# A two-layer gated cross-attention block: the first expert layer computed for every expert, and for the routed expert only

## The chip, the cores and the metric

One NeuronCore of one Trainium2 chip. The metric is the device time of one launch in microseconds. The kernel is written engine by engine: TensorE (PE), VectorE (DVE), ScalarE (ACT), GpSimd (POOL) and SyncE (SP), each with its own instruction order, and semaphores between them.

## The reference, cut to what matters

Eight batches of 256 rows of 256 numbers pass through two layers, each a gated cross-attention and a gated expert layer (`D` = 256, eight experts). Layer 0's expert layer takes one expert per row:

```python
x = x + tanh(g_xattn[0]) * L0_xattn(layernorm(x), ctx)      # bidirectional attention, one head, gated mix
x = x + tanh(g_ffn[0])   * L0_ffn(layernorm(x))
x = x + tanh(g_xattn[1]) * L1_xattn(layernorm(x), ctx, ctx) # 16 heads of 16, rotary embedding
x = x + tanh(g_ffn[1])   * L1_ffn(layernorm(x))             # 8 experts of 128, the best 2 per row

def L0_ffn(x):
    logits = x @ router_w.T + router_b
    probs = softmax(logits)
    top1 = argmax(probs)
    y_all = einsum('bsd,eod->bseo', x, expert_w) + expert_b
    return y_all[top1] * max(probs)
```

## The kernel before, in words

All of `x` stays on the chip in `xall` [128, 8, 2, 256]: batch, two row tiles of 128, 256 columns. Most products are made as three fp32r matmuls of a high and a low part (`mm3`, lines 298 to 301: hi*hi, hi*lo, lo*hi); so every operand is split, high part by ACT (`*_hi`), low part by DVE or POOL (`*_lo`). Weights are loaded by SP into one of four `stage` buffers, and split into `wA` (attention) or `wB` (the eight layer-0 experts, later layer 1's f and p).

The order of work is written out by hand, once per engine, as a list of calls under conditions on `k`. There are two loops. The first (`k` from -1 to 9) is a software pipeline of layer 0: iteration `k` makes the projections, scores and softmax of batch `k`, PV, gate, mix and the second layer norm ("B") with the routing of batch `k`-1, and the experts of batch `k`-2. `k` = 8 and 9 only drain it, and start layer 1's attention for batch 0 (`c_qk(0)` in `k` = 9). The second loop (`k` from 1 to 11) is layer 1: `c_qk`/`c_v` of batch `k`, `c_max` (scores once, for the row maxima) of batch `k`-1, `c_exp`/`c_PV` (scores again, transposed, with the maxima as three more rows of the contraction) of batch `k`-2, output projection and layer norm "D" of `k`-3, and the expert layer `d_up`/`d_down` of `k`-4. The last batch's experts 1 to 7 stand in its first iteration.

Layer 0's experts: `expert(x, b)` takes a pair of experts (`p = x // 2`) and one row tile (`t = x % 2`) and writes 128 rows by two experts' 256 columns, six matmuls of 512 columns. All eight experts are computed for all rows: eight calls per batch. `add_expert` on DVE (line 1221) then adds each expert's 256 columns to `xall`, scaled by `gat`, which is the softmax's maximum where the expert is the chosen one and zero elsewhere. The bias goes in as a product of the transposed gates with the eight bias rows (`gT`, `bias`, `add_bias`). `b_top` (DVE) picks the best expert.

Names for the steps below: `ln_apply` (line 1093) writes the normalized rows; `out_f`, `out_hi`, `out_lo` take PV from PSUM on ACT, DVE and POOL before `gate`; `sum_diff` (POOL) and `gated` (DVE) prepare `mix`; `mixed` adds it to `xall`. In layer 1 `swap_halves` (SP, line 1757) exchanges halves of q and k by DMA for the rotation, `turned` (DVE and POOL) rotates, `part0` to `part2` split into three bf16 parts, `stack` (SP, line 1770) copies them to `st_` with twelve DMAs, `max_parts` and `max_rows` (line 1777) bring the row maxima there with three. PSUM's eight banks are handed out in rings (`take`); a bank is waited for by its next taker.

## Time and profile before

| | us |
|---|---|
| median of 3 runs | 680.89 (680.26 to 686.58) |
| the profiled execution | 681.88 |
| its span, first to last instruction | 679.9 |
| busy in the span: PE / weight loads / DVE / ACT / POOL | 561.5 / 476.3 / 525.0 / 301.1 / 220.6 |
| instructions | 11549 |
| moved by DMA | 34.31 MB |

Busy times are unions of intervals. A matmul's listed duration is longer than its step to the next one, because matmuls are pipelined; the start of the next instruction tells what one costs. "[0.24 <-POOL rstd L1595]" behind an instruction is the idle time of its engine before it and the releaser. SPq is SP's DMA-issuing queue.

### The profile page before, as it was taken

The numbers are of one execution on the slowest core, as the hardware profiler recorded it, in microseconds if no ns is written. First come the engines' busy times: TensorE is split into PE (matmuls) and PEld (weight loads), VectorE is DVE, ScalarE is ACT, GpSimd is POOL, SyncE is SP. The second block draws the span as 40 slices with busy tenths as digits, with TensorE's granted clock in tenths as the row PEclk, the third lists the DMA queues.
The fourth block names the chain that finished last, engine by engine and source line by source line (L and its number), as shares of the span: only waits on it lengthen the run. The fifth ranks groups of instructions, "written<-read, shape, count | busy, mean of one in ns | idle before, by whom it ended". The sixth has DMA issues, their size and how long they took to land.

```text
span 679.9 us, 11549 instructions
## 1 busy us (share of the span) xinstructions
PE 561.5 (83%) x4240; PEld 476.3 (70%) x4240; DVE 525.0 (77%) x1279; ACT 301.1 (44%) x629; POOL 220.6 (32%) x225
## 2 busy tenths in 40 slices
PE   3778999999999999464646758889897988797977
PEld 3677899898999997353433545768685776676777
DVE  3688988888888779774746748797988969687576
ACT  2536343433343443121114637565655655455622
POOL 2340413222231303311605434452726344212123
PEclk9998999999999999797886879999999989899989
DMA  5233010101000100018184643508081451700000
GB/s 190 78 94 93 1 32 1 32 2 63 1 1 1 63 1 1 15 31 116 24 118 116 113 60 57 87 24 135 0 101 43 57 85 24 88 2 18 16 1 31
DMA packets 25720, 34.31 MB, mean 50 GB/s; under 512 B 3648, under 2 KB 16704, under 8 KB 25664
## 3 DMA queue, kind: packets, MB, share of 16 engines
q1 hardware_dynamic: 25664, 33.58, 25.8%
q8 instruction: 33, 0.54, 0.4%
q14 instruction: 23, 0.19, 0.1%
HBM read 14.50 MB, written 2.10 MB: 24 GB/s over the span
## 4 chain that ended last, share of the span: by engine, by line
PE 44%; DVE 21%; SPq 10%; DMA 8%; issue 8%; ACT 5%; POOL 4%; DVEq 0%; POOLq 0%; ACTq 0%
PE psum L299 12%; PE psum L301 12%; PE psum L300 12%; SPq L1770 8%; DMA st<-mpt 6%; DVE mpad L1246 4%; DVE xn L1093 4%; PE psum L306 2%; PE psum L462 2%; DVE xall L1334 2%; PE psum L447 2%; PE psum L473 1%; DVE qr L1231 1%; SPq L1777 1%; DVE wB L1069 1%
## 5 line engine op out<-in xcount | busy, mean ns | idle before, releaser
L1246 DVE TENSOR_REDUCE mpad<-psum 128x2 f32<-128x512 f32 x128 | 84.0, 682 | 43.7 <-PE psum L447 43.6
L852 ACT ACTIVATE PT<-psum 128x512 f32<-128x512 f32 x128 | 72.3, 595 | 33.9 <-PE psum L462 32.0
L462 PE MATMUL psum<-st 99*128 99x256 bf16 x256 | 47.5, 286 | 30.3 <-DMA st<-mpt 23.6
L447 PE MATMUL psum<-st 96*128 96x256 bf16 x256 | 50.7, 293 | 23.4 <-DVE mpad L1246 14.3
L1221 DVE SCALAR_TENSOR_TENSOR xall<-psum,gat,xall 128x256 f32<-128x256 f32 x128 | 61.3, 479 | 6.2 <-PE psum L301 3.3
L1642 POOL TENSOR_TENSOR wA<-stage,wA 128x512 fp32r<-128x512 f32 x24 | 30.8, 1283 | 88.9 <-ACT wA L890 64.2
L299 PE MATMUL psum<-wB,x2h 128*128 128x512 f32 x128 | 53.5, 418 | 1.0 <-DVE xall L1221 1.0
L447 PEld LDWEIGHTS psum<-st 96*128 96x128 bf16 x256 | 19.8, 104 | 45.4 <-DVE mpad L1246 29.4
L462 PEld LDWEIGHTS psum<-st 99*128 99x128 bf16 x256 | 19.7, 101 | 45.5 <-DMA st<-mpt 25.0
L1334 DVE SCALAR_TENSOR_TENSOR xall<-psum,gat,xall 128x256 f32<-128x256 f32 x112 | 47.9, 474 | 4.5 <-PE psum L301 3.3
L1093 DVE TENSOR_SCALAR xn<-xall,mv,rstd 128x256 f32<-128x256 f32 x64 | 46.3, 764 | 6.5 <-POOL rstd L1595 6.5
L301 PE MATMUL psum<-wB,x2l 128*128 128x512 f32 x128 | 51.1, 399 | 0.0
L300 PE MATMUL psum<-wB,x2h 128*128 128x512 f32 x128 | 51.1, 399 | 0.0
L1600 POOL TENSOR_TENSOR cl<-cx,ch 128x512 fp32r<-128x512 f32 x14 | 17.9, 1278 | 86.3 <-ACT ch L742 86.2
L1588 POOL TENSOR_SCALAR ve<-mv 128x2 f32<-128x2 f32 x32 | 6.9, 217 | 114.7 <-DVE mv L1077 114.7
L299 PE MATMUL psum<-wB,wA 128*128 128x256 f32 x128 | 41.8, 327 | 2.6 <-DVE xall L1334 2.3
L306 PE MATMUL psum<-ident,xn 128*128 128x128 f32 x128 | 21.0, 290 | 24.4 <-DVE xn L1093 24.4
L881 ACT ACTIVATE stage<-psum 128x512 f32<-128x512 f32 x32 | 19.1, 598 | 44.7 <-PE psum L301 44.5
L299 PE MATMUL psum<-x4h,wB 128*128 128x256 f32 x128 | 37.8, 295 | 0.1
L300 PE MATMUL psum<-wB,wA 128*128 128x256 f32 x128 | 36.7, 287 | 0.0
L473 PE MATMUL psum<-PT,vv 128*32 128x256 f32 x512 | 35.1, 393 | 1.6 <-ACT PT L852 1.5
L301 PE MATMUL psum<-wB,wA 128*128 128x256 f32 x128 | 36.5, 285 | 0.0
(237 smaller groups left out, 1938.6 us busy)
## 6 DMA issues: line engine op xcount, KB each, us to landing
st<-parts SPq DMA_DIRECT2D x96, 128.0 KB, 5.6
stage<-mats_d SPq DMA_DIRECT2D x29, 256.0 KB, 4.1
cx<-ctx_d SPq DMA_DIRECT2D x16, 256.0 KB, 2.8
qr<-qp SPq DMA_DIRECT2D x16, 256.0 KB, 5.1
xall<-x_d SPq DMA_DIRECT2D x8, 256.0 KB, 3.0
out_d<-xall SPq DMA_DIRECT2D x8, 256.0 KB, 4.4
st<-mpt SPq DMA_DIRECT2D x24, 8.0 KB, 5.7
rope<-rope_d SPq DMA_DIRECT2D x1, 256.0 KB, 3.0
```

Of the source, the lines that this page charges most:

```text
L299: e.matmul(out, lhs[0], rhs[0], start=start, stop=False)
L300: e.matmul(out, lhs[0], rhs[1], start=False, stop=False)
L301: return e.matmul(out, lhs[1], rhs[0], start=False, stop=stop)
L447: last = e.matmul(o[:, t * 256:(t + 1) * 256], s[0:96, 0, h, t * 128:(t + 1) * 128], s[0:96, 1, h, :], start=True, stop=True)
L462: last = e.matmul(o[:, k * 256:(k + 1) * 256], s[0:99, 1, h, k * 128:(k + 1) * 128], s[0:99, 0, h, :], start=True, stop=True)
L473: last = e.matmul(o[32 * j:32 * j + 32, c:c + 256], vv[b % 3][:, k, h, :], PT[:, (H * b + h) % 6, k, :], start=(k == 0), stop=(k == 1))
L852: e.activation(flat(PT[:, n % 6, :, :]), ps("ST", b, h), ACT.Exp, scale=0.25).then_inc(a_ST, 1)
L1093: last = e.tensor_scalar(xn[:, i, t, :], xall[:, b, t, :], mv[:, i, t, 0:1], rstd[:, i, t:t + 1], ALU.subtract, ALU.mult)
L1221: e.scalar_tensor_tensor(out=xall[:, b, t, :], in0=ps("ffn", b, x)[:, i * 256:(i + 1) * 256], scalar=gat[:, b % 2, t, 2 * p + i:2 * p + i ...
L1246: e.tensor_reduce(mpad[:, :, h:h + 1], ps("max", b, h).rearrange("p (a n) -> p a n", a=2), AX, ALU.max, negate=True).then_inc(v_max, 1)
L1334: e.scalar_tensor_tensor(out=xall[:, b, t, :], in0=ps("dn", b, x)[:, t * 256:(t + 1) * 256], scalar=gat[:, b % 2, t, x:x + 1], in1=xall[:, ...
L1770: e.dma_start(st_[b % 2][16 * c:16 * c + 16, i, :, :], parts[:, i, p, :, :].rearrange("p o n -> p (o n)")).then_inc(d_stack, 16)
```

## The change

Layer 0's rows are sorted by expert on the chip, in three groups of 2, 3 and 3 batches (`GROUPS`). `b_top` writes the one-hot choice to `oh`. `rank(g)` counts, by products with a triangular matrix and a matrix of ones, how many earlier rows chose the same expert; `alloc(g)` gives every expert as many tiles of 128 slots as it needs and every row its slot, and every tile its expert. POOL's `scatter(g)` writes the normalized rows to a DRAM buffer `slots_d` by indirect DMA (128 rows of 1 KB each). Then each of the group's `2n+7` tiles (11, 13 and 13, enough for any routing) is loaded (`xs`), with its expert's weights and bias (`wt`, 768 columns, picked by a register read from `tile_e`), transposed, multiplied in plain fp32 (`moe_T`, `xs_T`, `moe_w`), the bias added (`y_out`), and stored to `y_d`; `gather(b)` brings the rows back and `add_moe(b)` adds them to `xall`, scaled. Three buffers of each go round. Slots that no row fills are zero at the start (`zero_slots`). Routing of layer 0 is now a plain fp32 product (`route_B`) straight to rows by experts. The experts' split copies, `gpad`, `gT`, `bias` and `x_lo` of B are gone; the new tiles share SBUF with `wB`, which layer 1 fills later.

Both loops become one, `k` from -1 to 20, with a new order on every engine. PV and `out` of batch `k` now stand in iteration `k`, `proj("qc")` an iteration earlier; `c_qk(0)` stands in `k` = 8, `c_max` of batch `k`-9, `c_exp` of `k`-10, `c_out` of `k`-11, `d_up` of `k`-12. `rank`/`scatter`: `k` = 2/3, 6/6, 8/9. Tiles 0 to 10 are multiplied in `k` = 4 to 6, 11 to 23 in `k` = 6 to 8, 24 to 36 in `k` = 10 and 11. `gather`: 0 and 1 in `k` = 6, 2 and 3 in 8, 4 in 9, 5 to 7 in 11.

```diff
-            def expert(x, b, ring="all"):
-                o = take(ring, "ffn", b, x)
-                p, t = x // 2, x % 2
...
-                for k in range(2):
-                    last = mm3(o.rearrange("p (a n) -> p a n", a=2), hl(x2[b % 2], lambda a: a[:, k, t * 128:(t + 1) * 128]),
-                               hl(wB, lambda a: a[:, 2 * p:2 * p + 2, k * 256:(k + 1) * 256]), k == 0, k == 1)
...
+GROUPS = [2, 3, 3]
+ROWT = [2 * n for n in GROUPS]
+TILES = [n + E - 1 for n in ROWT]
...
+            def rank(g, ring="all"):
+                o = take(ring, "rank", g)
+                w.wait_ge(v_oh, FIRST[g + 1])
...
+                e.matmul(o[:, 0:n * E], tri[:, :], oh[:, g, 0:n, :].rearrange("p a e -> p (a e)"), start=True, stop=False)
+                for i in range(ROWT[g]):
+                    last = e.matmul(o[:, (i + 1) * E:n * E].rearrange("p (a e) -> p a e", e=E), ones[:, :],
+                                    oh[:, g, i:i + 1, :].broadcast_to([128, n - 1 - i, E]), start=False, stop=(i == n - 2))
+            def moe_T(n, ring="all"):
+                o = take(ring, "moe", n)
+                w.wait_ge(d_xs[n % 3], 16 * (n // 3 + 1))
+                for k in range(2):
+                    last = e.transpose(o[:, k * 128:(k + 1) * 128], xs[:, n % 3, k * 128:(k + 1) * 128], ident[:, :])
+            def moe_w(n):
+                o = ps("moe", n)
+                w.wait_ge(a_xs, n + 1)
+                w.wait_ge(d_wt[n % 3], 16 * (n // 3 + 1))
+                for k in range(2):
+                    last = e.matmul(o[:, 256:512], xsT[:, n % 2, k, :], wt[:, n % 3, k * 256:(k + 1) * 256], start=(k == 0), stop=(k == 1))
+            def y_out(n):
+                w.wait_ge(t_moe, n + 1)
+                w.wait_ge(d_ys[n % 3], 16 * (n // 3))
...
+                e.tensor_tensor(ys[:, n % 3, :], ps("moe", n)[:, 256:512], wt[:, n % 3, 512:768], ALU.add).then_inc(v_ys, 1)
+            def add_moe(b):
+                w.wait_ge(d_yg[b % 2], 32 * (b // 2 + 1))
+                w.wait_ge(p_gat, 2 * b + 2)
+                for t in range(2):
+                    e.scalar_tensor_tensor(out=xall[:, b, t, :], in0=yg[:, b % 2, t, :], scalar=gatB[:, b, t:t + 1], in1=xall[:, b, t, :],
+                                           op0=ALU.mult, op1=ALU.add).then_inc(v_acc, 1)
+            def scatter(g):
+                w.wait_ge(v_slot, g + 1)
+                w.wait_ge(d_zero, 32)
+                w.wait_ge(t_xs, TILE0[max(g - 1, 0)])
+                for i in range(ROWT[g]):
+                    e.indirect_dma_start(slots_d[g % 2][0:128 * TILES[g], :], bass.IndirectOffsetOnAxis(ap=slot[:, g, i:i + 1], axis=0),
+                                         xB[:, (FIRST[g] + i // 2) % 5, i % 2, :], None).then_inc(d_slots, 16)
+            def gather(b):
+                g = GROUP[b]
+                for i in range(3):
+                    w.wait_ge(d_ys[i], 16 * ((TILE0[g + 1] + 2 - i) // 3))
+                w.wait_ge(v_acc, 2 * (b - 1))
+                for t in range(2):
+                    i = 2 * (b - FIRST[g]) + t
+                    e.indirect_dma_start(yg[:, b % 2, t, :], None, y_d[g % 2][0:128 * TILES[g], :],
+                                         bass.IndirectOffsetOnAxis(ap=slot[:, g, i:i + 1], axis=0)).then_inc(d_yg[b % 2], 16)
+            def load_tile(n):
+                g, j = tile_at(n)
+                w.wait_ge(v_tile, 2 * g + 2)
+                w.wait_ge(v_ys, n - 2)
+                at = e.value_load(tile_e[0:1, g, j:j + 1], min_val=0, max_val=E - 1)
+                e.dma_start(wt[:, n % 3, :], exp_d[bass.ds(at, 1), :, :].rearrange("a p n -> p (a n)")).then_inc(d_wt[n % 3], 16)
+                w.wait_ge(d_slots, 32 * FIRST[g + 1])
+                w.wait_ge(t_xs, n - 2)
+                e.dma_start(xs[:, n % 3, :], slots_d[g % 2][128 * j:128 * (j + 1), :]).then_inc(d_xs[n % 3], 16)
+            def store_tile(n):
+                g, j = tile_at(n)
+                w.wait_ge(v_ys, n + 1)
+                w.wait_ge(v_acc, 2 * FIRST[max(g - 1, 0)])
+                e.dma_start(y_d[g % 2][128 * j:128 * (j + 1), :], ys[:, n % 3, :]).then_inc(d_ys[n % 3], 16)
```

`alloc(g)` is twelve small DVE operations on [128, 64] to [128, 104] numbers. On DVE `st0_init` (the memset of `st_[0]`, before on POOL) and `vv_init` stand in `k` = 8, and the one-hot vectors of both routings are made by one comparison with the index itself, without a cast.

## Rows read from the trace of the kernel before

**Rows 1.** The page's 40 slices of the span: busy tenths and granted clock.
```profile
PE   3778999999999999464646758889897988797977
...
DVE  3688988888888779774746748797988969687576
...
PEclk9998999999999999797886879999999989899989
```
**Rows 2.** Six stretches: PE, PEld, DVE, ACT, POOL busy (count), clock, DMA share, GB/s.
```profile
33.40:61.80 28.40, 21.66 (x173) 20.33 (x173) 22.88 (x49) 15.06 (x37) 7.88 (x9) 1.00 0.26 77
128.90:161.30 32.40, 32.40 (x229) 29.89 (x228) 28.51 (x76) 12.53 (x32) 8.23 (x10) 1.00 0.06 18
262.40:324.50 62.10, 34.48 (x186) 28.73 (x184) 43.05 (x85) 14.07 (x30) 17.50 (x16) 0.86 0.30 50
324.50:358.70 34.20, 18.87 (x104) 13.51 (x104) 20.80 (x39) 5.80 (x11) 12.54 (x11) 0.85 0.48 73
358.70:398.20 39.50, 26.17 (x194) 17.85 (x194) 24.85 (x45) 20.11 (x39) 18.15 (x17) 0.80 0.61 114
461.30:500.00 38.70, 34.08 (x304) 27.18 (x303) 33.68 (x81) 23.29 (x44) 18.22 (x18) 1.00 0.40 63
```
**Rows 3.** PE in order of time: a projection, an `expert`, `mix` (start, us).
```profile
141.19 0.28 PE L299 MATMUL psum<-ch,wA 128*128 128x256 f32 x1
...
142.59 0.39 PE L299 MATMUL psum<-wB,x2h 128*128 128x512 f32 x1
...
144.00 0.60 PE L382 MATMUL psum<-ident,uu 128*128 128x128 f32 x4
144.35 0.36 PE L299 MATMUL psum<-ch,wA 128*128 128x256 f32 x1
```
**Rows 4.** A group of the page (`add_expert`), and one `c_PV` on PE.
```profile
L1221 DVE SCALAR_TENSOR_TENSOR xall<-psum,gat,xall 128x256 f32<-128x256 f32 x128 | 61.3, 479 | 6.2 <-PE psum L301 3.3
...
480.57 1.07 PE L473 MATMUL psum<-PT,vv 128*32 128x256 f32 x16
```
**Rows 5.** DVE in order of time: first and last of `b_top`, `gT_lo`, `add_bias`.
```profile
128.86 0.17 DVE L1161 COPY lg<-psum 128x16 f32<-128x16 f32 x1
...
131.30 0.17 DVE L1197 COPY gpad<-gat 128x16 f32<-128x16 f32 x1
...
135.69 0.41 DVE L1201 TENSOR_TENSOR gTl<-psum,gTh 128x256 fp32r<-128x256 f32 x1
...
141.49 0.68 DVE L1207 TENSOR_TENSOR xall<-psum,xall 128x512 f32<-128x512 f32 x1
```
**Rows 6.** One row each of POOL and ACT, and two `ln_apply` on DVE.
```profile
134.75 1.30 POOL L1605 TENSOR_TENSOR cs1l<-cf,cs1h 128x512 fp32r<-128x512 f32 x1 [0.66 <-DVE cs1h L1141]
...
134.99 0.39 ACT L811 ACTIVATE gTh<-psum 128x256 fp32r<-128x256 f32 x1 [0.78 <-PE psum L405]
...
138.12 2.67 DVE L1093 TENSOR_SCALAR xn<-xall,mv,rstd 128x256 f32<-128x256 f32 x2 [0.24 <-POOL rstd L1595]
...
148.60 0.73 DVE L1093 TENSOR_SCALAR xn<-xall,mv,rstd 128x256 f32<-128x256 f32 x2
```
**Rows 7.** Weight conversions on DVE before the experts start, and PE's wait behind them.
```profile
57.94 2.50 DVE L1069 TENSOR_TENSOR wB<-stage,wB 128x512 fp32r<-128x512 f32 x4
...
61.78 0.56 PE L299 MATMUL psum<-PT0h,vsh 128*128 128x256 f32 x1 [2.46 <-DVE PT0l L1135]
```
**Rows 8.** `c_qk(0)`, SP's issues of `stack(0)`, the first `c_max`, SP's `max_rows(0)`.
```profile
290.75 0.28 PE L299 MATMUL psum<-xh,wA 128*128 128x256 f32 x1
...
309.20 8.39 SPq L1770 DMA_DIRECT2D st<-parts  x12
...
324.52 0.61 PE L447 MATMUL psum<-st 96*128 96x256 bf16 x2 [8.21 <-DMA st<-parts]
...
353.10 1.86 SPq L1777 DMA_DIRECT2D st<-mpt  x3
```
**Rows 9.** The page's row for the weight loads: count, KB each, us to landing.
```profile
stage<-mats_d SPq DMA_DIRECT2D x29, 256.0 KB, 4.1
```

More of the change, by code:

```diff
@@ new lines, in tensor_program @@
+                if 0 <= k - 10 < NB:
+                    c_exp(0, k - 10)
+                if k == 8:
+                    ln_T("C", "all", 1)
+                if 1 <= k - 8 < NB:
+                    c_v(k - 8, "g")
+                if k == 4:
+                    moe_w(2)
+                if 0 <= k - 9 < NB:
+                    c_max(1, k - 9)
+                if k == 7:
+                    ln_T("C", "all", 0)
+                if k == 10:
+                    moe_T(25, "g")
+                if k == 7:
+                    moe_T(20)
@@ new lines, in tensor_program @@
+                if 0 <= k - 9 < NB:
+                    c_max(4, k - 9)
+                if 0 <= k - 10 < NB:
+                    c_PV(0, k - 10)
+                    c_exp(5, k - 10)
+                if k == 10:
+                    moe_T(28, "g")
+                    moe_w(28)
+                if 0 <= k - 10 < NB:
+                    c_exp(6, k - 10)
+                if 0 <= k - 12 < NB:
+                    d_down(3, k - 12)
+                if k == 10:
+                    moe_T(29, "g")
@@ new lines, in tensor_program @@
+                if 0 <= k - 9 < NB:
+                    c_max(8, k - 9)
+                if 0 <= k - 10 < NB:
+                    c_exp(9, k - 10)
+                if 0 <= k < NB:
+                    PV(0, k)
+                if k == 10:
+                    moe_w(30)
+                if 0 <= k - 11 < NB:
+                    top_D(k - 11)
+                if 0 <= k - 9 < NB:
+                    c_max(9, k - 9)
+                if k == 10:
+                    moe_T(31, "g")
+                if k == 8:
+                    rank(2)
```

2035 lines of the change are left out of this document (1221 added, 814 removed).

## The prediction, made before the changed kernel was run

> **What bounds the kernel now.** I read the slices of the span first, then stretches cut at the kernel's own borders, then single instructions inside one iteration. The slices show two stages [rows 1]: until about 265 us TensorE (PE) is at 9 tenths nearly everywhere, afterwards PE and DVE share the load at 4 to 9 tenths and the granted clock dips. The stretches say it in microseconds [rows 2]. One layer-0 iteration with experts (128.9 to 161.3) takes 32.4 us and PE is busy all of it, DVE 28.5: PE is the bound, DVE close behind. The iteration before the experts start (33.4 to 61.8) takes 28.4 with PE busy 21.7: waits between engines bound it. The hand-over to layer 1 (262.4 to 324.5) is 62.1 us with PE 34.5, and its last wait is for a DMA [rows 8]. A steady layer-1 iteration is 38.7 with PE 34.1 and DVE 33.7, both near full; the two before it (34.2 and 39.5) are looser.
>
> **Part 1: what leaves.** One `expert` call is six 512-column matmuls, start to next start 142.59 to 144.00, 1.41 us; the twelve 256-column ones of a projection take 141.19 to 142.59, 0.12 each [rows 3]. 64 expert calls are 90 us of PE, per batch 11.3, plus bias and routing (12 of 0.12) and 0.25 of transposes. DVE loses 16 accumulations of 0.48 per batch [rows 4], 7.7 us; a bias add (0.68), `x_lo` of B (as large, 0.68), `gTl` (0.41) and some 1.5 of the 2.6 that `b_top` takes from 128.86 to 131.47 [rows 5]: 10.9 per batch, 87 in all, and 7 us of weight conversions.
>
> **Part 2: what comes.** A tile of 128 slots costs PE two transposes (0.09 each: four take 144.00 to 144.35 [rows 3]) and two true fp32 matmuls of 256 columns. The nearest row is `c_PV`: eight fp32 calls of 256 columns, four side by side in the array, recorded as 16 instructions in 1.07 us [rows 4]: two groups after each other, 0.5 each. So 1.0 for the pair and 1.2 per tile. Below: 0.24 at the fp32r rate of rows 3; above: 2.0 if nothing overlaps. The Trainium skill (FP8 and Floating Point Precision) says true FP32 takes four passes through the array; four times 0.12 is 0.48 per matmul, so rule and row agree, and the change pays a quarter-rate matmul where the old code paid three full-rate ones. There are 4+7, 6+7, 6+7 = 37 tiles for 16 row tiles, whatever the routing: 44 us. The work does not fall to an eighth but to a half: PE gains 90+8-44-3 (routing and ranks) = 51 us. DVE: `y_out` like `gTl` 0.41 x 37 = 15, `add_moe` 16 x 0.48 = 8, `alloc` 3 x 3 (a dozen operations of 0.17 to 0.3), net 62 less. ACT: 37 copies of 0.39 [rows 6] are 14 more on an engine whose busiest layer-0 stretch has 15.1 of 28.4 [rows 2], hidden. POOL: 16 scatters and 16 gathers, which no row shows; from 0.6 (an issue on SP [rows 8]) to 2.7 (twice a 1.3 us POOL operation [rows 6]). I take 1.3, 42 us, on an engine busy 8.2 of 32.4 in layer 0 and 18.2 of 38.7 in layer 1 [rows 2].
>
> **Part 3: layer 0, what is late next.** Without experts PE needs 32.4-11.3-1.65+0.4 = 19.9 per iteration. The row for an iteration without experts is 28.4; its last 3 us are DVE converting four expert weights from 57.94, for which `PV` waits [rows 7], so 25.4. Walking the new order with the durations of rows 5 and 6, I find waits of 1.2 at `mix` (2.7 us of `ln_apply` A beside POOL [rows 6] sit ahead of `gated`), 0.4 and 0.5 at the scores, 1 at `P_T(1)`, 1.2 at the two `PV`: 24. Seven periods from the end of `PV(1,0)` to the end of `PV(1,7)` are 168; the 20 tiles in them add 24 of PE work, of which the 4 us of waits per iteration hide a third: 16; two `alloc`, two scatters ahead of `ln_rstd` B on POOL: 4. Together 188. Before, `PV(0,0)` starts at 33.4 and `PV(1,0)` ends 3.7 later (twice 1.4 and a wait); 262.4-37.1 = 225. **Gain 37** (bounds: +29 at PE's floor, -10 at 25.4).
>
> **Part 4: hand-over.** Before, `PV(1,7)` to the first `c_max` is 62.1; `c_qk(0)` starts only at 290.75 [rows 8], 33.8 before the end of it, being an iteration later. Now `c_qk(0)` stands in iteration 8 behind `gate(7)`, two tiles and `mix(7)`: 3+2.9+2+1 = 9 us. The 33.8 stay (projections, swap by DMA, rotation, twelve stack DMAs issued in 8.4 us from 309.20, landed at 324.52 [rows 8]) plus 2 for `st0_init` and `b_top` ahead of `turned` on DVE. 45: **gain 17**. `rank(2)`, `alloc(2)` and six scatters (8 us at 1.3) run beside the stack DMAs: nothing. The next stretch (34.2) loses seven expert adds on DVE: **gain 3**.
>
> **Part 5: what the tiles of group 2 cost layer 1.** Iteration 10 answers to 358.7 to 398.2. It gets 11 loads (two DMAs and a register load each) and 11 stores on SP, in order, ahead of `stack(2)` and `max_rows(1)`. SP issues a small DMA in 0.6 and a stack DMA in 0.7 [rows 8]. A buffer comes round after issue 1.7, landing 5 (256 KB take 4.1 [rows 9], this is 384 KB), transpose, copy, matmuls, add 2.0 and handovers 0.8: 9.5 per three tiles. Ten tiles from 27 on take 32, then `stack(2)` 8.4, three max rows 1.9 and 5 to land follow: 47 and more after `c_exp(0,0)`, with the lead-in 52. **Loss 12.5** (bounds 0, where it hides in SP's old idle time, and 40, at a landing of 14). A register load on SP is in no row; 0.3 to 2 each, the second adds 14. Iterations 11 and 12 take gathers 5 to 7 with POOL's rotation work behind them, and the f and p weights: **loss 4**. In the steady ones `d_top` drops a cast and two one-hot operations, 1 us of DVE: **gain 5**.
>
> By the fit in the Trainium skill (DMA: Bandwidth & Descriptors, Anatomy of one DMA), 2.0 us plus bytes over 436 GB/s, the 384 KB would land in 2.9, an estimate; the sum would be 7 us lower.
>
> **Sum.** 37+17+3-12.5-4+5 = 45.5. The profiled execution took 681.88 with a span of 679.9; 679.9-45.5+2.0 = 636.4; the median shown (680.89) lies 1.0 below the profiled run, so 635.5.
>
> **Rivals.**
> *Shorter iterations.* If the new order lets PE run at its floor of about 20 plus tiles, part 3 gains 25 more: 610. For it: all waits I found are under 1.3 us. Against: DVE needs 18.6 of the 24 and is used in strict order.
> *The tile ring becomes the bound (the slower side).* Three buffers, one SP queue, DMAs in order. Place: iterations 4 to 8 and 10 to 11. If a load lands in 14 us instead of 5 (the last of twelve piled-up stack DMAs landed 15.3 after the first issue, rows 8), a tile takes 6.2 us: 14 tiles in iterations 5 and 7 take 87 instead of 59, 13 in iteration 10 and 11 take 81 instead of 52, the others 12 more: +69, 704. It decides from about 5 us more per round trip on, where the 45 are eaten. Against: DMA is at 0.06 in the layer-0 stretch [rows 2].
> *The clock falls in layer 0.* PE at 80% busy instead of 100. In rows 2 stretches with PE at 55 to 66% had a granted clock of 0.80 to 0.86, those with 76 and 88% had 1.00. If a quarter of layer 0 ran at 1.2 instead of 2.4 GHz, 38 us of PE work come back: 673.
> The Trainium skill (TensorE: Matmul & The Clock Gate, Part 1) says that the throttled state is the default and activity releases it; by that rule a layer 0 with gaps is at risk, and the trace agrees only for the looser stretches.
> *POOL's indirect DMAs are slow.* `scatter(1)` and `gather(0)` stand ahead of `ln_rstd` B(5), the gathers 5 to 7 ahead of `turned(0,3)`. In rows 6 the DVE pair that takes 0.73 alone takes 2.67 beside POOL, so the two disturb each other. At 2.7 each: +10 in iteration 6, +5 in 3, +7 in 11: 658. Together with a tempo 2 us per tile worse: the gain is gone.
> The Trainium skill (DMA: Bandwidth & Descriptors, SWDGE vs HWDGE vs iDMA) says POOL writes its descriptors into SBUF and DVE's 2-port mode locks it out of that; no row here shows such a DMA.
> *The change is only half of what it says* is in the sum: 37 tiles at quarter rate.
>
> **Chances.** Forecast (620 to 655) 0.45; shorter iterations 0.2; clock 0.08; slow indirect DMAs 0.1; gain eaten, within 1%, 0.05; tile ring slower than before 0.12. A measurement tells this kernel from no change at about 1%. Faster 0.83, same 0.05, slower 0.12. The range reaches from 602 (shorter iterations and a cheap iteration 10) to 674 (clock); what lies beyond is mostly the tile ring.
>
> **What would show it.** Right: `PV(1,7)` ending near 225, layer-0 periods near 24 without tiles and 29 with seven; the first `c_max` near 270; iteration 10 near 52; PE busy about 50 and DVE about 60 us lower; a `moe_w` pair of 1.0. Wrong: waits of PE for DMA xs or wt in iterations 5 and 7 (tile ring); granted clock under 0.95 before 225 (clock); PE waiting for xB behind `ln_rstd` B in iteration 6 (indirect DMAs); `c_max` waiting for stack DMAs that SP issued late in iteration 11.

## The result and the profile after

The changed kernel takes 664.5 us (median of 4 runs, 662.0 to 665.9), the kernel before, on the same chip, 683.7 (4 runs, 680.3 to 687.3). The ratio is 0.9715, 95% interval 0.9643 to 0.9786: faster by 2.85%, 19.2 us. The forecast was a gain of 45.5 us. The sign held, and 664.5 lies inside the outer range of 602 to 674, but above the 620 to 655 that had the largest chance: less than half of the gain came. Medians here are over all executions of a kernel; the ratios leave out the single ones that ran in a slower state of the chip.

Two rows of the page of the changed kernel, and its granted clock, answer to [rows 1]:

```profile
PE   3899879999878965545668767989888999898977
...
DVE  3787876767846688755433675898988889787476
...
PEclk9899989999989998666798957999999899899989
```

Layer 0 now ends in the 15th slice instead of the 16th, but behind it, in slices 17 to 25, the granted clock is mostly 5 to 8 tenths. Busy in the span: PE 528.5 us (33 less, forecast 51), DVE 466.1 (59 less, forecast 62). These are the stretches, cut where [rows 2] were cut; the columns are the same. First five layer-0 iterations from one `PV(1)` to the next (2, 3, 4, 5 and 6 by the batch of `PV`), then, behind the dots, the hand-over, the stretch from the first maximum to the first exponential, iteration 10 and iteration 11:

```profile
57.10:81.20 24.10, 21.61 (x172) 20.43 (x172) 19.30 (x49) 11.46 (x33) 9.26 (x12) 1.00 0.06 21
81.20:111.10 29.90, 24.87 (x183) 23.88 (x183) 21.02 (x61) 11.47 (x33) 13.42 (x16) 0.89 0.28 91
111.10:137.60 26.50, 24.71 (x192) 23.49 (x193) 20.94 (x52) 12.06 (x35) 9.27 (x12) 1.00 0.09 28
137.60:168.90 31.30, 29.04 (x217) 27.02 (x215) 20.71 (x55) 14.61 (x42) 9.26 (x12) 1.00 0.56 173
168.90:204.10 35.20, 28.20 (x208) 26.58 (x208) 22.86 (x67) 12.55 (x36) 18.66 (x21) 0.95 0.33 102
...
237.20:289.60 52.40, 27.89 (x159) 25.09 (x157) 34.77 (x72) 13.01 (x31) 26.14 (x28) 0.74 0.56 119
289.60:322.20 32.60, 16.46 (x70) 9.30 (x71) 17.58 (x33) 5.40 (x12) 11.81 (x11) 0.64 0.72 134
322.20:373.20 51.00, 38.99 (x268) 28.26 (x268) 24.44 (x49) 20.23 (x43) 11.83 (x11) 0.93 0.70 189
373.20:424.70 51.50, 38.75 (x271) 27.47 (x271) 34.60 (x79) 26.62 (x50) 29.58 (x28) 0.73 0.45 93
```

An iteration without tiles takes 24.1, as walked. Those with tiles, slots or gathers take 26.5 to 35.2; iteration 10 takes 51.0 (forecast 52), and iteration 11, which took 36.1 before (398.9 to 435.0), takes 51.5.

The page's rows for the new work. The first two are groups (instructions, busy us, mean ns, idle before them), the others DMA issues (count, KB each, us to landing):

```profile
L1443 DVE TENSOR_TENSOR ys<-psum,wt 128x256 f32<-128x256 f32 x37 | 15.4, 418 | 40.9 <-PE psum L435 37.2
L435 PE MATMUL psum<-wt,xsT 128*128 128x256 f32 x148 | 41.2, 407 | 3.4 <-ACT xsT L939 3.2
...
wt<-exp_d SPq DMA_DIRECT2D x37, 384.0 KB, 3.7
```

So `y_out` takes 0.42 (taken: 0.41), the pair of `moe_w` 41.2 / 37 = 1.1 over all clocks (taken: 1.0), and a load lands in 3.7 (taken: 5). At a granted clock of 1.00 a pair takes 0.87, from its start to that of the next instruction:

```profile
149.22 1.03 PE L435 MATMUL psum<-wt,xsT 128*128 128x256 f32 x4
150.09 0.38 PE L427 MATMUL psum<-ident,xs 128*128 128x128 f32 x2
```

The parts were priced near what they cost. What was not is where they stand.

### The profile page after: what moved, and what is told of

Its sections match the earlier page's. It is cut to its first block, busy times and chain, and to the rows that moved or that the text cites. A ratio compares the mean times of both kernels' runs of the same rounds, so it can differ in the third digit from the quotient of the medians.

```text
span 660.7 us, 11514 instructions
## 1 busy us (share of the span) xinstructions
PE 528.5 (80%) x4052; PEld 446.2 (68%) x4052; DVE 466.1 (71%) x1120; ACT 298.3 (45%) x665; POOL 260.9 (39%) x283
## 4 chain that ended last, share of the span: by engine, by line
PE 36%; DVE 20%; POOL 12%; issue 11%; DMA 10%; SPq 6%; ACT 5%; POOLq 0%; DVEq 0%; ACTq 0%
PE psum L313 8%; PE psum L315 7%; PE psum L314 7%; DMA xs<-slots_d 4%; SPq L2138 3%; PE psum L435 3%; PE psum L498 2%; DMA st<-parts 2%; DVE oh L1387 2%; PE psum L487 2%; POOL qp L1915 2%; PE psum L472 2%; DMA stage<-mats_d 2%; PE psum L320 2%; DVE mpad L1507 2%
## 5 line engine op out<-in xcount | busy, mean ns | idle before, releaser
L978 ACT ACTIVATE PT<-psum 128x512 f32<-128x512 f32 x128 | 73.3, 594 | 31.5 <-PE psum L487 31.0
L472 PE MATMUL psum<-st 96*128 96x256 bf16 x256 | 53.7, 306 | 29.5 <-DMA st<-parts 18.3
L1934 POOL TENSOR_TENSOR wA<-stage,wA 128x512 fp32r<-128x512 f32 x24 | 33.5, 1397 | 95.0 <-ACT wA L1017 55.1
L1595 DVE SCALAR_TENSOR_TENSOR xall<-psum,gat,xall 128x256 f32<-128x256 f32 x112 | 47.7, 475 | 9.5 <-PE psum L315 8.4
L313 PE MATMUL psum<-wB,wA 128*128 128x256 f32 x128 | 40.3, 315 | 6.3 <-DVE xl L1306 4.3
L1443 DVE TENSOR_TENSOR ys<-psum,wt 128x256 f32<-128x256 f32 x37 | 15.4, 418 | 40.9 <-PE psum L435 37.2
L435 PE MATMUL psum<-wt,xsT 128*128 128x256 f32 x148 | 41.2, 407 | 3.4 <-ACT xsT L939 3.2
L1008 ACT ACTIVATE stage<-psum 128x512 f32<-128x512 f32 x32 | 19.1, 598 | 49.7 <-PE psum L315 49.7
L487 PEld LDWEIGHTS psum<-st 99*128 99x128 bf16 x256 | 19.1, 100 | 32.2 <-ACT PT L978 20.9
L313 PE MATMUL psum<-x4h,wB 128*128 128x256 f32 x128 | 39.6, 309 | 1.3 <-DVE xall L1595 0.8
L1301 DVE TENSOR_SCALAR xn<-xall,mv,rstd 128x256 f32<-128x256 f32 x48 | 28.9, 644 | 12.8 <-POOL rstd L1887 12.8
L314 PE MATMUL psum<-x4l,wB 128*128 128x256 f32 x128 | 37.6, 294 | 0.0
L315 PE MATMUL psum<-x4h,wB 128*128 128x256 f32 x128 | 37.5, 293 | 0.0
L314 PE MATMUL psum<-wB,wA 128*128 128x256 f32 x128 | 36.0, 281 | 0.0
L315 PE MATMUL psum<-wB,wA 128*128 128x256 f32 x128 | 35.9, 280 | 0.0
L320 PE MATMUL psum<-ident,xn 128*128 128x128 f32 x96 | 17.0, 306 | 20.1 <-DVE xn L1301 20.1
L435 PEld LDWEIGHTS psum<-wt,xsT 128*128 128x128 f32 x148 | 27.1, 202 | 8.5 <-ACT xsT L939 5.9
```

The source lines that it names most:

```text
L313: e.matmul(out, lhs[0], rhs[0], start=start, stop=False)
L314: e.matmul(out, lhs[0], rhs[1], start=False, stop=False)
L315: return e.matmul(out, lhs[1], rhs[0], start=False, stop=stop)
L320: last = e.transpose(o[:, k * 256 + t * 128:k * 256 + t * 128 + 128], src[:, t, k * 128:(k + 1) * 128], ident[:, :])
L435: last = e.matmul(o[:, 256:512], xsT[:, n % 2, k, :], wt[:, n % 3, k * 256:(k + 1) * 256], start=(k == 0), stop=(k == 1))
L472: last = e.matmul(o[:, t * 256:(t + 1) * 256], s[0:96, 0, h, t * 128:(t + 1) * 128], s[0:96, 1, h, :], start=True, stop=True)
```

## Experiments: what the added work costs

"Changed" is the changed kernel as given. All times are medians, of four executions, and of six in the last four runs; each ratio is to runs of the kernel before beside it (683 to 686 us). Stage lengths come from one profiled execution each, and they scatter: iteration 10 takes 51.0 us in the changed kernel, and 55.6 and 51.7 in the two runs of part 3, whose edits do not touch it.

**1. Everything added left out (called bare).** The order of work stays. The calls do nothing, each in the program of its engine (put together here), and the waits for their results are gone too.

```diff
+            rank = moe_T = moe_w = xs_T = alloc = y_out = add_moe = lambda *a: None
+            scatter = gather = zero_slots = load_tile = store_tile = lambda *a: None
```

> Leaves out all that the change adds and keeps its order of work: no counting, no slots written or read, no tiles, no adding back (the first FFN's output is missing, its router and gates stay). Theory A, the added work costs more than the 36.5 us of my sum (16 tiles + 4 slots in layer 0, 12.5 in iteration 10, 4 in iterations 11 and 12), and what the removal gives was right: about 602 us, so that the added work costs 62. Theory B, the added work costs the 36.5 us, and the removal gives less than the 82 us that I reckoned: about 628 us. Layer-0 periods near 24 us all through by both.

Measured: 600.7 us, ratio 0.879 (0.876 to 0.883). The same kind of rows for this kernel: all of layer 0's seven periods, hand-over, maxima, iterations 10 and 11, the rest:

```profile
32.40:201.50 169.10, 151.18 (x1204) 142.89 (x1204) 133.49 (x337) 81.56 (x234) 64.73 (x84) 1.00 0.08 24
202.90:248.80 45.90, 18.00 (x110) 16.37 (x109) 26.97 (x49) 11.71 (x27) 14.32 (x15) 0.74 0.39 58
248.80:282.80 34.00, 18.22 (x79) 11.70 (x78) 17.44 (x30) 5.71 (x12) 12.17 (x11) 0.60 0.59 89
282.80:319.80 37.00, 26.33 (x195) 17.25 (x195) 21.80 (x43) 16.15 (x31) 13.75 (x13) 0.82 0.54 84
319.80:364.00 44.20, 34.94 (x272) 27.00 (x271) 27.07 (x65) 26.64 (x50) 23.52 (x20) 0.87 0.44 79
364.00:599.30 235.30, 206.40 (x1808) 167.71 (x1806) 190.05 (x463) 128.42 (x241) 93.61 (x91) 0.99 0.29 45
```

Theory A. The removal alone is worth 83 us, where my sum had 82; the added work costs 64 and not 36.5. Side by side (the forecast's loss of 4 in iterations 11 and 12 is split evenly here):

| us | before | forecast | bare | changed |
|---|---|---|---|---|
| start of `PV(1,0)` to start of `PV(1,7)` | 225.4 | 188 | 169.1 | 202.7 |
| end of `PV(1,7)` to the first maximum | 62.8 | 45 | 45.9 | 52.4 |
| to the first exponential of element 0 | 34.2 | 31 | 34.0 | 32.6 |
| iteration 10 | 39.5 | 52 | 37.0 | 51.0 |
| iteration 11 | 36.1 | about 38 | 44.2 | 51.5 |
| the rest | 244.9 | 242 | 235.3 | 236.0 |

(The lead-in, up to `PV(1,0)`, gives 2.5 in the changed kernel, 3.2 in bare, that I had not counted.) Walk (168 against 169.1) and hand-over (45 against 45.9) stand. The total of the removal stands partly by luck: iteration 11 of bare is 8.1 longer than before, where I had nothing, and the lead-in (3.2), iteration 10 (2.5) and the rest (9.6, reckoned 5) make up for it. What was under-priced is the added work in layer 0 (33.6 where I took 20), in the hand-over (6.5 for nothing) and in iteration 11 (7.3 more than bare, and bare itself 8 more than before). The next runs take these places one by one.

**2. How much is PE's own work, how much the loads.** Two kernels: `moe_w` takes only half of the contraction (the output lacks the other half); or ten tiles load no weights (they are multiplied by those of other tiles).

```diff
-                for k in range(2):
-                    last = e.matmul(o[:, 256:512], xsT[:, n % 2, k, :], wt[:, n % 3, k * 256:(k + 1) * 256], start=(k == 0), stop=(k == 1))
+                last = e.matmul(o[:, 256:512], xsT[:, n % 2, 0, :], wt[:, n % 3, 0:256], start=True, stop=True)
```

> Each tile's product takes the first half of the contraction only, one matmul instead of two (the first FFN's output is missing the other half). 37 x 0.5 us of PE at full clock less. Theory E, the tiles' PE time comes on top undiminished, in layer 0 and in iteration 10: -12 us at the end of PV(1,7) (24 tiles), -5 to -7 in iteration 10, about 645 in all. Rival F, in layer 0 a third of it had been hidden in waits as I forecast, and iteration 10 is set by the ring of tile buffers and SP's queue: -8 in layer 0 and -1 in iteration 10, about 655.

```diff
-                w.wait_ge(d_wt[n % 3], 16 * (n // 3 + 1))
+                w.wait_ge(d_wt[n % 3], 16 * min(n // 3 + 1, 9))
...
-                at = e.value_load(tile_e[0:1, g, j:j + 1], min_val=0, max_val=E - 1)
-                e.dma_start(wt[:, n % 3, :], exp_d[bass.ds(at, 1), :, :].rearrange("a p n -> p (a n)")).then_inc(d_wt[n % 3], 16)
+                if n < 27:
+                    at = e.value_load(tile_e[0:1, g, j:j + 1], min_val=0, max_val=E - 1)
+                    e.dma_start(wt[:, n % 3, :], exp_d[bass.ds(at, 1), :, :].rearrange("a p n -> p (a n)")).then_inc(d_wt[n % 3], 16)
```

> From tile 27 on no expert weights are loaded (these ten tiles are multiplied with what the three buffers hold, so the FFN's output of elements 5 to 7 is wrong): 3.8 MB, ten DMAs and ten register loads less in iteration 10. Rival F, iteration 10 (51.0 us) is set by the ring (issue, landing, copy, product, add and back) and by DMA traffic: -5 to -8 us, about 658. Theory E, it is set by PE's work: under 2 us, about 663.

Half the product: 662.3 (ratio 0.970). `PV(1,7)` starts 2.6 us sooner (233.2, not 235.8), iteration 10 takes 51.3. So neither E nor F in layer 0: halving the product saves 0.4, 1.2 and 1.1 us in iterations 4, 5 and 7 with 3, 7 and 6 products. The whole tile costs 1.03 in iteration 5 ((31.3 - 24.1) / 7), and that is PE's own time: PE is busy 29.0 us there and 21.6 in an iteration of bare, and idle 2.3 and 2.5. With half of the product it is busy 26.8 and idle 3.3. So half of what the product gave back went into waits that stand close behind it; which of them, was not tried. Iteration 10 is F's.

Weights kept: 651.3 (ratio 0.954), 13 less, more than F gave. Iteration 10 takes 42.1 instead of 51.0. The DMA row of its ten loads of rows (count, KB each, us to landing), first in the changed kernel, then in this one:

```profile
xs<-slots_d SPq DMA_DIRECT2D x10, 128.0 KB, 4.2
```
```profile
xs<-slots_d SPq DMA_DIRECT2D x10, 128.0 KB, 2.1
```

The same ten loads of rows land in half the time. To tell bytes from issue, a third kernel still issues the ten weight DMAs, but with 16 KB:

```diff
-                e.dma_start(wt[:, n % 3, :], exp_d[bass.ds(at, 1), :, :].rearrange("a p n -> p (a n)")).then_inc(d_wt[n % 3], 16)
+                c = 768 if n < 27 else 32
+                e.dma_start(wt[:, n % 3, 0:c], exp_d[bass.ds(at, 1), :, 0:c].rearrange("a p n -> p (a n)")).then_inc(d_wt[n % 3], 16)
```

> From tile 27 on the DMA of the expert weights is still issued, with its register load, but carries 32 of 768 columns (16 KB instead of 384 KB; the FFN's output of elements 5 to 7 is wrong). The run without these DMAs took 42.1 us in iteration 10 instead of 51.0. Theory F1, bytes: the 3.8 MB fill the 16 DMA engines beside the stack's copies (busy share 0.65 to 0.73 there): iteration 10 near 43, the end near 652. Theory F2, SyncE: issue and register load, about 0.8 us per tile in a queue that everything else of the iteration stands in: iteration 10 at 49 to 51, the end near 663.

652.5 us (ratio 0.9545, 0.950 to 0.959); iteration 10 takes 44.4. Bytes, F1: by these single profiles the issue and the register load are worth 2.3 us (44.4 - 42.1), the 3.7 MB 6.6 (51.0 - 44.4); the medians agree (1.1 us between the two kernels, 12 to the changed one). My working of iteration 10 (issue 1.7, landing 5, chain 2.8, three buffers) gave ten tiles 32 us; from the first weight load's issue at 323.3 to the tenth's at 354.8 they took 31.5. That is closer than the working deserves: with the landing of 4.2 that these loads had it gives 29, and 7.6 us lie between the eighth issue and the ninth alone.

**3. Waits that stand in a queue.** In iterations 3 and 6 slots are written by POOL ahead of `ln_rstd` B. These rows of the changed kernel are POOL's in iteration 6, and PE's wait behind them:

```profile
184.68 0.96 POOL L1961 DMA_INDIRECT slots_d<-xB,slot  x1 [0.30 <-issue]
185.94 0.98 POOL L1971 DMA_INDIRECT yg<-y_d,slot  x1 [0.30 <-issue]
187.23 0.95 POOL L1971 DMA_INDIRECT yg<-y_d,slot  x1 [0.30 <-issue]
188.21 0.23 POOL L1884 TENSOR_SCALAR ve<-mv 128x2 f32<-128x2 f32 x1
```
```profile
190.16 1.08 PE L320 MATMUL psum<-ident,xB 128*128 128x128 f32 x4 [3.72 <-DVE xB L1301]
```

The last of eight indirect DMAs, 1.27 each with its issue, ends at 188.2; `xB` follows, and PE has stood 3.7 us.

```diff
 GpSimd, iteration 3
-scatter(0); ln_rstd("B", 2)
+ln_rstd("B", 2); scatter(0)
 GpSimd, iteration 6
-scatter(1); gather(0); ln_rstd("B", 5)
+scatter(1); ln_rstd("B", 5); gather(0)
```

> GpSimd's ln_rstd B stands ahead of scatter(0) in iteration 3, and gather(0) behind ln_rstd B and ahead of rex_in in iteration 6 (scatter(1) stays ahead). Theory A, the in-order queue: -1 to -2 us in iteration 3 (period 29.9) and -2.5 us in iteration 6 (35.2), about 660.5. Rival B, VectorE's alloc ahead of ks's low part and the tiles themselves set these periods: unchanged within 1 us, about 664.

662.9 (ratio 0.968, 0.963 to 0.973; changed 0.9715): no difference that can be told. The wait did go, from 3.7 to 1.2 us, and iteration 6 took 35.7 all the same. The granted clock shows why. Columns: stretch, length, PE busy (count), clock, DMA share, GB/s. First changed, then this kernel, then the combined kernel of part 5, which has the same edit in iteration 6:

```profile
190.20:193.00 2.80, 2.80 (x14) 0.50 0.88 271
```
```profile
185.00:188.00 3.00, 1.11 (x8) 1.00 0.43 101
188.00:195.30 7.30, 7.30 (x38) 0.53 0.48 158
```
```profile
187.00:190.00 3.00, 1.22 (x9) 1.00 0.40 127
190.00:193.00 3.00, 3.00 (x28) 1.00 0.88 253
```

With the shorter waits the clock fell all the same, and stayed at its lower level (1.2 GHz) for 7 us where it had been 3; that took back what the wait gave. Where it held at 2.4 GHz, iteration 6 took 32.4, 2.8 us less than in the changed kernel (35.2). Why it held in one and not in the other, no row tells.

The same in iteration 3, where PE waits 2.67 us for the low part of `ks`, which stands behind `alloc(0)` on VectorE, and then has a granted clock of 0.51 for 6.1 us (94.9 to 101.0):

```diff
 VectorE, iteration 3
-alloc(0); proj_lo("ks", 3); mixed(2); proj_lo("qs", 3); row_max(0, 3)
+proj_lo("ks", 3); mixed(2); proj_lo("qs", 3); row_max(0, 3); alloc(0)
 GpSimd, iteration 3: as above
```

> Iteration 3 only: VectorE's alloc(0) stands behind row_max(0) instead of ahead of ks's low part, and scatter(0) behind ln_rstd B. In the changed kernel PE waited 2.7 us for ks's low part there and then ran 6 us at a granted clock of 0.50. Theory C, a short wait costs twice, once as a wait and again as half clock behind it: the wait goes and the clock stays at 1.00, the period of iteration 3 (29.9) falls to about 25, the end by 4 to 5 us, about 660. Rival D, the half clock belongs to the work of rank(0) just before and comes all the same: the period falls by at most 1 to 2 us and the end by under 2, about 663. The run before with scatter(0) alone moved left the period at 29.9.

The clock stayed at 1.00 all through iteration 3, which fell from 29.9 to 27.2. Theory C, at half its size: a wait of 2.0 us came in place of the other, now for the last row of `alloc`. The total is 664.9 (0.971, 0.959 to 0.983), no difference to the changed kernel that can be told: iteration 6 took 38.2 in this profile.

**4. The first maximum.** In the changed kernel PE's first `c_max` starts at 285.5, when the stack has landed; DVE takes it at 289.6:

```profile
289.57 0.69 DVE L1507 TENSOR_REDUCE mpad<-psum 128x2 f32<-128x512 f32 x1 [6.82 <-POOL mpad L1977]
```
```profile
288.17 0.97 POOL L1961 DMA_INDIRECT slots_d<-xB,slot  x1 [0.30 <-issue]
289.14 0.33 POOL L1977 MEMSET mpad<- 128x256 f32 x1
```

A memset of 0.33 us, which waits only for layer 0's last `mix` and routing, stands behind two gathers and six scatters.

```diff
 GpSimd, iteration 9
-gather(4); scatter(2); mpad_init(); turned(0, 1)
+mpad_init(); gather(4); scatter(2); turned(0, 1)
```

> The memset of mpad stands ahead of gather(4) and scatter(2) on GpSimd in iteration 9 instead of behind them. Theory A: the first head_max falls from 289.6 to the landing of the stack near 286, and the end by 3 to 4 us, about 661. Rival B, the maxima are paced by what else stands in iteration 9 (value copy, rotation, stack(1)) and the gain is absorbed before the first exponential: under 1 us, about 664.

The hand-over fell from 52.4 to 48.6, as theory A had it, but the end did not: 667.7 us (0.9765, 0.972 to 0.981). Iteration 10 took 58.9 us; PE waited 10.1 us for `xs` in it instead of 7.0, at a granted clock of 0.84 instead of 0.93. That the earlier arrival caused this is not shown, for iteration 10 also took 55.6 without this edit, in the first run of part 3; and the combined kernel of part 5, which has the edit, kept the hand-over at 48.9 with an iteration 10 of 46.7.

**5. Iteration 11, five runs.** ScalarE's and POOL's rows in the changed kernel:

```profile
375.15 0.59 ACT L978 ACTIVATE PT<-psum 128x512 f32<-128x512 f32 x1
383.73 0.63 ACT L962 ACTIVATE parts<-qp 128x512 bf16<-128x512 f32 x1 [7.99 <-POOL qp L1915]
```
```profile
375.81 1.12 POOL L1971 DMA_INDIRECT yg<-y_d,slot  x1 [0.17 <-issue]
377.23 1.26 POOL L1971 DMA_INDIRECT yg<-y_d,slot  x1 [0.31 <-issue]
378.79 0.95 POOL L1971 DMA_INDIRECT yg<-y_d,slot  x1 [0.30 <-issue]
380.04 0.95 POOL L1971 DMA_INDIRECT yg<-y_d,slot  x1 [0.30 <-issue]
381.02 1.27 POOL L1912 TENSOR_TENSOR qp<-qp,rope 128x512 f32<-128x512 f32 x1
```

The exponentials stand 8 us behind `part0`, which stands behind four indirect DMAs. The rival that I gave 0.1 named this very place, but made it hang on slow DMAs; at 1.3 each it is there already.

```diff
 GpSimd, iteration 11
-gather(5); gather(6); turned(0, 3); gather(7); ln_rstd("C", 4); turned(1, 3)
+turned(0, 3); ln_rstd("C", 4); turned(1, 3); gather(5); gather(6); gather(7)
 VectorE: add_moe(5), (6), (7) behind head_max(9) (second run: at the end)
 ScalarE: the f weights' casts wait for the last tile, not for the adding back
```

> In iteration 11 the gathers of elements 5, 6 and 7 stand behind GpSimd's turned(1, 3) instead of ahead of turned(0, 3), their adding back behind head_max(9), and the f weights' casts wait for the last tile instead of for the adding back. Theory A, the in-order queue of GpSimd: ScalarE stood 8.0 and 3.0 us for the rotated q and k with the softmax's exponentials behind them, 5.2 and 2.9 us of it gathers: iteration 11 (51.4 us) falls by 6 to 8 us, and 664.5 goes to about 657.5. Rival B, iteration 11 is bound by the loads of the stacks and row maxima behind the tiles' DMAs: unchanged within 1 us, about 664.

> As the run with the gathers behind turned(1, 3), and the adding back of elements 5 to 7 now at the very end of VectorE's iteration 11, behind the routing of layer 1 (there ScalarE had then waited 6.5 us for VectorE, which stood at the adding back). Theory A, the stall had only moved from one in-order queue to the next: iteration 11 falls from 51.4 us to about 45, the 44.2 that it takes without any added work, and the end by 5 to 6, about 658. Rival B, iteration 11 is bound by the half clock (0.6 granted in its first half) whatever stalls: over 50 us, no change at the end.

664.2 (0.975, 0.969 to 0.982) and 666.7 (0.977, 0.969 to 0.985). Iteration 11 took 53.5 and 54.3: rival B in effect, though no run tested its reasons. The stall had moved: first ScalarE waited 6.5 us for layer 1's routing on VectorE, which stood at the adding back; then 8.7 for the adding back itself, ahead of the p weights' cast.

The next run aimed at the end of iteration 10. The rows of tile 36 landed beside the stack's DMAs, and the last maxima of element 1 stood behind them on PE. SyncE's issues in the changed kernel:

```profile
356.74 7.76 SPq L2138 DMA_DIRECT2D st<-parts  x12
369.26 1.99 SPq L2145 DMA_DIRECT2D st<-mpt  x3
```

It was through with the stack at 364.5 and stood 4.8 us for these maxima. The edit is made to the kernel with gathers and adding back last:

```diff
 TensorE, iterations 10 and 11
-moe_T(35); c_max(14, 1); moe_T(36); moe_w(35); c_max(15, 1); c_out(0); moe_w(36); c_maxT(1)
+c_max(14, 1); c_max(15, 1); c_out(0); c_maxT(1); moe_T(35); moe_T(36); moe_w(35); moe_w(36)
 VectorE: y_out(35), y_out(36) behind max_parts(1)
```

> As the run with the gathers and the adding back last, and tiles 35 and 36 (transposes, products, bias) now behind c_maxT(1) on PE and behind max_parts(1) on VectorE; in that run the rows of tile 36 took 7.5 us to land beside the stack's twelve DMAs, and the last maxima of element 1 stood behind them. Theory G, the in-order queue of PE behind the last tiles' loads ends iteration 10: it falls from 54.9 to 48 or less, the end by 5 or more from 666.7. Rival H, the maxima would then wait for something else (buffers of the maxima, VectorE, half clock): under 2 us.

658.1 (0.967, 0.963 to 0.971), 8.6 us below the kernel it is made from, though the two intervals still touch; iteration 10 took 46.1, where that kernel had 54.9 and the changed kernel 51.0, and SyncE went from the stack to the maxima without a pause (361.7 to 361.8). Theory G. Then everything together, the edits of this run, of iterations 3 and 9 and `gather(0)` behind `ln_rstd` B:

> All the moves together: alloc(0) and scatter(0) late in iteration 3, gather(0) behind ln_rstd B in iteration 6, the memset of mpad first in iteration 9, tiles 35 and 36 behind c_maxT(1), gathers 5 to 7 and their adding back last in iteration 11. If the single gains (2.8 in iteration 3, 4 at the first maxima, 5 to 7 in iteration 10, 3 to 6 in iteration 11) add up: about 650. If each is given back at the next wait or in half clock, as in the single runs so far: 660 to 666.

656.2 (0.962, 0.959 to 0.966), 2.0 below the last, which is within the noise: little of the single gains added up. Iteration 11 took 53.7. One more order of its end:

```diff
 VectorE, iteration 11
-d_top(0); ...; w_lo("f1"); add_moe(5); add_moe(6); add_moe(7); head_max(12, 2)
+d_top(0); add_moe(5); add_moe(6); ...; w_lo("f1"); head_max(12, 2); add_moe(7)
 ScalarE, iterations 11 and 12
-w_hi("p0"); w_hi("p1"); st_exp(15, 1)
+st_exp(15, 1); w_hi("p0"); w_hi("p1")
```

> As the combined kernel, with the end of iteration 11 sorted once more: the adding back of elements 5 and 6 behind d_top(0) on VectorE, that of element 7 behind head_max(12), and ScalarE's casts of p0 and p1 behind the last exponential of element 1 instead of ahead of it. In the combined kernel ScalarE stood 8.5 us for the adding back of element 7, with that exponential behind it, and PE 9.9 us for the exponential; iteration 11 took 53.7 us. Theory A, that stall is the whole excess over the 44.2 us without added work: iteration 11 falls to 44 to 47 and the end to 647 to 650. Rival B, iteration 11 has now had its stall on three engines in turn (GpSimd, VectorE, ScalarE) and will show a fourth: over 50 us, the end above 653.

656.0 (0.958, 0.954 to 0.961): no gain. Rival B: iteration 11 took 55.0 us, with the fourth stall (ScalarE again stood 7.2 us for the adding back). But every version has one thing in common. These rows are ScalarE's casts of the f and p weights (`wB<-stage`) and the first gelu of layer 1 (`stage<-psum`). Before:

```profile
364.29 1.13 ACT L717 ACTIVATE wB<-stage 128x512 fp32r<-128x512 f32 x2
...
382.93 1.14 ACT L717 ACTIVATE wB<-stage 128x512 fp32r<-128x512 f32 x2
422.98 0.60 ACT L881 ACTIVATE stage<-psum 128x512 f32<-128x512 f32 x1
```

Changed:

```profile
393.01 0.62 ACT L849 ACTIVATE wB<-stage 128x512 fp32r<-128x512 f32 x1
...
408.74 0.63 ACT L849 ACTIVATE wB<-stage 128x512 fp32r<-128x512 f32 x1 [0.40 <-DMA stage<-mats_d]
412.09 0.60 ACT L1008 ACTIVATE stage<-psum 128x512 f32<-128x512 f32 x1
```

Before, the last two of the eight matrices are cast 16 us ahead of the first exponential of iteration 11 (398.9). Now they lie where the tile buffers were, so they come after the last tile, within the iteration (373.2 on), in two rounds through four staging buffers; and the gelu needs these buffers. From the first cast to the first gelu it is 19.1 us, in bare 19.2.

**6. The passage of the weights.** First the gathered rows `yg` get memory of their own, so that the p casts need not wait for the adding back:

```diff
-        yg = sm_("yg", [128, 2, 2, 256])
+        yg = sb("yg", [128, 2, 2, 256])
...
                 if n[0] == "p":
-                    w.wait_ge(v_acc, 2 * NB)
+                    for i in range(3):
+                        w.wait_ge(d_ys[i], 16 * ((TILE0[NG] + 2 - i) // 3))
```

> As the second combined kernel, but the gathered rows (yg, 4 KB per partition) lie outside the memory that layer 1's p weights take over; so ScalarE's casts of the p weights wait for the last tiles' stores and no longer for the adding back of element 7. In all versions with tiles the first gelu came 19 us after the first f cast where nothing stood between (bare 11.1 to 30.3, changed 19.8 to 38.9, in us from the first exponential of the iteration), and 29 us after it where the p casts waited for the adding back (12.2 to 41.1). Theory K, this chain sets iteration 11: first gelu at 31 to 33, iteration 11 at 45 to 47 instead of 55.0, the end near 648. Rival L, something else of the iteration (half clock, VectorE) is as late: over 51 us, the end above 653.

658.8 (0.963, 0.959 to 0.968), iteration 11 took 54.1: rival L. The casts now waited for their loads:

```profile
396.61 0.63 ACT L850 ACTIVATE wB<-stage 128x512 fp32r<-128x512 f32 x1 [6.93 <-DMA stage<-mats_d]
400.63 0.63 ACT L850 ACTIVATE wB<-stage 128x512 fp32r<-128x512 f32 x1 [3.39 <-DMA stage<-mats_d]
```

which SyncE issued only at 393.8, when the low part of f1, late in VectorE's order and 6.65 us long instead of 0.68 (see the last section), had freed its buffer. So these moved forward too:

```diff
 ScalarE, iteration 11
-w_hi("f0"); ...; w_hi("f1"); ...; w_hi("f2"); ...; w_hi("f3")
+w_hi("f0"); ...; w_hi("f1"); w_hi("f2"); w_hi("f3")
 VectorE, iteration 11
-w_lo("f0"); ...; w_lo("f1")
+w_lo("f0"); w_lo("f1")
 GpSimd, iteration 11
-turned(1, 3); gather(5); gather(6); gather(7); ...; w_lo("f2"); w_lo("f3")
+turned(1, 3); w_lo("f2"); w_lo("f3"); gather(5); gather(6); gather(7)
```

> As the kernel with yg apart, with the casts of f2 and f3 directly behind that of f1 on ScalarE, the low part of f1 directly behind that of f0 on VectorE, and those of f2 and f3 ahead of the gathers on GpSimd; so the staging buffers come free some 10 us earlier for p1 to p3. Theory M, the passage of the eight matrices through the staging buffers sets iteration 11: first gelu at 29 to 33 us instead of 40.2, iteration 11 at 44 to 48 instead of 54.0, the end at 649 to 652 instead of 658.8. Rival L, something else is as late (maxima, half clock, gathers now 2.6 us later on GpSimd): over 51 us, the end above 655.

650.8 us (649.3 to 653.9), ratio 0.953 (0.949 to 0.957): 8 us below the run before it, 4.7% below the kernel before and 14 us below the changed one; from the second combined kernel (0.958, 0.954 to 0.961) it can't be told for certain. The total fell where theory M had it, but partly by luck: iteration 11 took 49.9 (expected 44 to 48) and the first gelu came at 37.3 us (29 to 33), neither theory's numbers. Of the 9.1 us between the two profiles 4.2 are iteration 11's; 3.8 are iteration 10's (50.6 and 46.8), which the edit does not touch.

That the passage of the weights sets iteration 11 is better shown by the rows of all runs together. Before the first gelu ScalarE loads a table, and what that waits for is the last low part of the weights, on POOL, in the changed kernel:

```profile
410.80 1.28 ACT L1008 ACT_TABLE_LOAD   x1 [1.43 <-POOL wB L1874]
```

It is so in all 15 kernels with the new order. Seven of them, in us from the start of iteration 11:

| | first cast | last cast | first gelu | end |
|---|---|---|---|---|
| bare | 11.1 | 26.4 | 30.3 | 44.2 |
| changed | 19.8 | 35.5 | 38.9 | 51.5 |
| gathers late | 13.2 | 37.5 | 40.9 | 53.5 |
| combined | 13.4 | 37.3 | 41.1 | 53.7 |
| second combined | 12.3 | 37.8 | 41.1 | 55.0 |
| `yg` apart | 11.8 | 36.8 | 40.2 | 54.1 |
| weights early | 11.9 | 33.5 | 37.3 | 49.9 |

In all 15 the gelu comes 3.3 to 3.9 us behind the last cast and the end 12.6 us behind the gelu, or 13.9 in three of them. So what moved the last cast moved the end. In the changed kernel the first cast stood behind ScalarE's waits for the rotated q and k (8.0 and 3.0 us), and the last adding back, for which it has to wait too, ended only 0.4 us before it. In the four runs listed next the first cast went some 7 us earlier, but the p casts waited for the adding back or for their loads, and the last cast came no sooner.

## Why the prediction was right and wrong

- **Part 1, what leaves: right in layer 0 and the hand-over,** and in the total (83 us, forecast 82) with the luck told in experiment 1. The walked period of 24 is 24.0 to 24.1, the hand-over of bare 45.9 (45). The rival *shorter iterations* fell with that.
- **Part 2, what comes: right piece by piece.** 1.1 for the pair (0.87 at full clock), 0.42 for `y_out`, 1.27 for an indirect DMA and its issue in a row of them. DVE fell by 59 (62). PE fell by 33 instead of 51. Bare has 475.2 us of it: the removal took 86 and not 98, the added work brings 53 and not 47. 37 pairs at 1.1 busy us instead of 1.0 are 4 of these 6; and from the hand-over to iteration 11 (clock 0.60 to 0.87 in bare, 0.80 to 0.94 before) the same matmuls count as busy for longer.
- **Part 3, the step that failed first: "of which the 4 us of waits per iteration hide a third".** Nothing was hidden: in iteration 5 PE's idle time is 2.3 us with seven tiles and 2.5 without. Of the 33.6 us (202.7 - 169.1) the 20 tiles in the seven periods took 20.8 and not 16 (+4.8), 1.04 each. And "two `alloc`, two scatters ahead of `ln_rstd` B on POOL: 4" measured 5.8 in iteration 3 (29.9 - 24.1) and 35.2 - 24.1 - 4 x 1.03 = 7.0 in iteration 6, 12.8 in all (+8.8). The in-order waits behind these small instructions were the larger error, and moving them got back 2.7 us in iteration 3 and 2.8 in iteration 6 where the clock held. A wait of 2.7 or 3.7 us of PE there was followed by 6.1 and 2.8 us at half clock. The rival *clock falls in layer 0* was right in kind, at a cost near 4 us instead of 38, an estimate: half of the 5.5 and 2.8 us that PE was busy in them.
- **Part 4: "beside the stack DMAs: nothing" failed.** Against bare it cost 6.5: 3.4 us by the memset behind the scatters (DVE's first maximum starts 4.0 after PE's `c_max`, 0.6 in bare), 1.9 by a later landing of the stack (17.0 us from the first issue at 268.6 to PE's first `c_max`, 15.0 in bare), and 1.1 by that issue itself. The gain of 3 in the stretch behind it was 1.6.
- **Part 5: iteration 10 right in number, 51.0 against 52, and in half of its mechanism.** The loads do set it (42.1 without the weights), by the ring and SyncE's queue, though not at the landing of 5 that I took. But 4.8 us of it SyncE stood for maxima behind the last two tiles on PE, which are in no term of mine; with the two tiles moved it took 46.1. On the other side the landing of 4.2 gave back about 3, an estimate by the working in experiment 2 (32 and 29). That the number fitted so well is luck.
- The 2.9 us by the fit that the Trainium skill gives (DMA: Bandwidth & Descriptors, Anatomy of one DMA), an estimate, would have made the ring too quick; the page gives the fit for DMAs issued from GpSimd, and these were SyncE's. No run shows such a load alone: wt landed in 3.7, and 4.2 in iteration 10. The same `xs` loads took 4.2 beside the weights and 2.1 without them. The register load, in no row before, takes 0.3 us, and 0.7 to 0.8 from its start to the issue of the load behind it.
- **"Iterations 11 and 12 take gathers 5 to 7 ..., and the f and p weights: loss 4" failed most.** Iteration 11 alone lost 15.4. I named the weights and never asked when they could be converted before. 8 of the 15.4 come without any tile: bare has the new order and the weights in iteration 11. The other 7 are the gathers and what waits behind them: the first cast comes at 19.8 us into the iteration and in bare at 11.1, and the gelu at 38.9 and at 30.3.
- The rival *tile ring* left small marks: PE waited for `xs` 0.5 us in iteration 5 and 1.2 in iteration 7. It decided nothing in layer 0. *Slow indirect DMAs* named the right places, iterations 3, 6 and 11, at a price of 2.7 that they did not have.
- Of what was to be seen: `PV(1,7)` ended at 237 (225), the first `c_max` at 285.5 (270), a clock under 0.95 before 225 and PE waiting for `xB` in iteration 6 were both there.
